# Six attention and feed-forward layers on one core: the weighted values are computed transposed, and the weights are divided by their sums before them

## The reference

```python
sim = jnp.einsum('bhwie,bhwje->bhwij', bq, bk2) * QK_SCALE   # 32 queries x 64 keys
sim = jnp.where(mask, -jnp.finfo(sim.dtype).max, sim)
attn = jax.nn.softmax(sim, -1)
out = jnp.einsum('bhwij,bhwje->bhwie', attn, bv2)
...
return out.transpose(0, 2, 1, 3).reshape(b, n, INNER) @ Wo
```

## Time and profile before

| | |
|---|---|
| median of 3 runs | 3407.45 us |
| the profiled execution, its own time | 3406.7 us |
| its span | 3405.0 us |
| TensorE matmul busy | 3269.8 us, 96% |
| VectorE busy | 2966.7 us, 87% |
| ScalarE busy | 2734.6 us, 80% |
| GpSimd busy | 2616.7 us, 77% |
| granted TensorE clock, mean | 0.988 |

### The profile page before, as it was taken

How to read it: one execution, slowest core, us unless ns; L and a number is a source line. 1 busy time by engine, 2 the same in 40 slices (tenths; PEclk the granted TensorE clock), 3 DMA queues, 4 the chain that set the end, 5 groups by cost and what they waited for, 6 DMA issues and landing times.

```text
span 3405.0 us, 161393 instructions
## 1 busy us (share of the span) xinstructions
PE 3269.8 (96%) x66106; PEld 2794.3 (82%) x66106; DVE 2966.7 (87%) x5352; ACT 2734.6 (80%) x4522; POOL 2616.7 (77%) x3360
## 2 busy tenths in 40 slices
PE   7999679999999999999999999999999999999996
PEld 5767458888888888888888888888888888888885
DVE  7777578999999999989999899999999999999995
ACT  4777458888888888888888888888888888888884
POOL 5677567777877777877778887788777878878774
PEclk9999889999999999999999999999999999999998
DMA  2000013222233222233222332222232222232221
GB/s 61 5 8 8 16 51 101 70 66 69 67 81 98 65 70 65 75 80 90 71 64 73 80 93 69 66 69 74 76 92 69 67 74 74 69 94 66 74 75 51
DMA packets 161952, 228.51 MB, mean 67 GB/s; under 512 B 42297, under 2 KB 60673, under 8 KB 161665
## 3 DMA queue, kind: packets, MB, share of 16 engines
q1 hardware_dynamic: 161792, 226.85, 24.8%
HBM read 21.00 MB, written 4.19 MB: 7 GB/s over the span
## 4 chain that ended last, share of the span: by engine, by line
POOL 38%; issue 32%; PE 15%; POOLq 2%; DVE 1%; ACT 1%; SPq 0%; DVEq 0%; ACTq 0%; DMA 0%
POOL by_cos L1253 12%; POOL by_cos L1259 9%; POOL newton_b L1239 2%; POOL newton_b L1241 2%; POOL norms L1243 2%; POOL newton_b L1237 2%; POOL xs_lob L1267 2%; POOL xn_lob L1278 2%; PE ring L1376 2%; POOL f_rstdb L1291 2%; PE ring L1430 2%; PE score L1395 1%; PE ring L1416 1%; PE proj L1367 1%; POOLq L1059 1%
## 5 line engine op out<-in xcount | busy, mean ns | idle before, releaser
L1253 POOL TENSOR_TENSOR by_cos<-by_cos,by_sin 128x1024 f32<-128x1024 f32 x384 | 914.4, 2391 | 0.0
L1259 POOL TENSOR_TENSOR by_cos<-by_cos,norms 128x1024 f32<-128x1024 f32 x384 | 729.8, 1912 | 0.0
L1653 DVE TENSOR_TENSOR by_cos<-proj,turns 128x512 f32<-128x512 f32 x768 | 524.3, 683 | 71.9 <-ACT squares L1539 67.4
L1367 PE MATMUL proj<-qkv_hi,xs_hib 128*128 128x512 f32 x1152 | 559.9, 486 | 25.6 <-DVE by_sin L1655 12.9
L1655 DVE TENSOR_TENSOR by_sin<-proj,turns 128x512 f32<-128x512 f32 x768 | 522.0, 680 | 0.0
L1539 ACT ACTIVATE squares<-proj 128x512 f32<-128x512 f32 x768 | 442.7, 593 | 41.4 <-DVE sumsb L1659 16.1
L1659 DVE TENSOR_REDUCE sumsb<-squares 128x16 f32<-128x1024 f32 x384 | 464.2, 1209 | 0.0
L1369 PE MATMUL proj<-qkv_hi,xs_lob 128*128 128x512 f32 x1152 | 457.2, 397 | 0.0
L1368 PE MATMUL proj<-qkv_lo,xs_hib 128*128 128x512 f32 x1152 | 456.7, 396 | 0.0
L1376 PE MATMUL ring<-ident,by_cos 128*128 128x128 f32 x3072 | 405.5, 275 | 7.8 <-ACT pTb L1518 4.5
L1376 PEld LDWEIGHTS ring<-ident,by_cos 128*128 128x128 f32 x3072 | 351.4, 141 | 56.4 <-issue 9.4
(11 more groups left out here) (191 smaller groups left out, 7846.5 us busy)
## 6 DMA issues: line engine op xcount, KB each, us to landing
v_win<-vb SPq DMA_DIRECT2D x1152, 128.0 KB
v_win<-vb SPq DMA_DIRECT2D x768, 64.0 KB
in_qkv<-L_ffn_Wqkv SPq DMA_DIRECT2D x12, 768.0 KB
wo<-L_ffn_Wo SPq DMA_DIRECT2D x6, 512.0 KB, 4.0
x_tok<-L_attn_x SPq DMA_DIRECT2D x8, 256.0 KB, 4.4
residual<-x_tok SPq DMA_DIRECT2D x8, 256.0 KB, 2.0
in_w<-L_ffn_W SPq DMA_DIRECT2D x12, 170.5 KB
in_qkv<-residual SPq DMA_DIRECT2D x1, 1536.0 KB, 7.3
```

What stands on the lines that cost most here:

```text
L1253: nc.gpsimd.tensor_tensor(both, both, by_sin[:, j, :], ALU.add).then_inc(e[f"{w_}_added"].sem, 1)
L1259: nc.gpsimd.tensor_tensor(heads, heads, inverse, ALU.mult).then_inc(e[f"{w_}_ready"].sem, 1)
L1367: nc.tensor.matmul(out, xs_hi[:, tile], qkv_hi[:, cols], start=True, stop=False)
L1653: nc.vector.tensor_tensor(of_heads(by_cos[:, t % 2, j, cols]), heads, table(0), ALU.mult)
```

## The change

`V` has its operands swapped. The values of a window and head are now stationary (64 rows and 64 columns of the array), the exponentials move over 32 columns, and there are again 64 such matmuls a tile. The result comes out with the features on the partitions, which is what `W` needs. `O` with its eight transposes, `R` and `attnb` are gone; `EO` copies straight from the result of `V`. Since the queries no longer lie on the partitions of the result, the division by the sums has moved ahead: a new VectorE step `PN` multiplies `probs` by the reciprocals into `weightsb`, all in SBUF, and `X` transposes `weightsb`. `SB` now waits for `PN` of the tile before (not `X`), `PN` waits for `X` of the tile before. `VM` waits for the scores of its own tile, not of the one before. `Wo` is laid out by heads and loaded with two DMAs instead of one. All tables of order are new; `X` of a pass's first tile is now done one pass later.

```diff
-    "Pool": "Mk:0 XSd:2 Ak:1 N:1 FP XSd:3 Mq:1 XL Mk:1 Xl Aq:2 N:2 Ak:2 Aq:3 Mq:2",
+    "Pool": "XSd:2 N:1 Mq:1 Mk:1 XSd:3 FP Aq:2 XL N:2 Xl Ak:2 Aq:3 Mk:2 Ak:3 Mq:2",
...
-RELEASE = {"Tq": ("q_T", 1), "Tk": ("k_T", 1), "X": ("pT", 1), "V": ("attn", 1), "O": ("oT", 1), "W": ("x_mid", 1),
+RELEASE = {"Tq": ("q_T", 1), "Tk": ("k_T", 1), "X": ("pT", 1), "V": ("oT", 1), "W": ("x_mid", 1),
...
-                    wait_tile(sp, "s_full", t - 1, when)
+                    wait_tile(sp, "s_full", t, when)
...
                 elif kind == "X":
                     out = take(token, kind, t, when)
-                    wait_tile(pe, "exp", t, when)
+                    wait_tile(pe, "weights", t, when)
                     for i in range(PAIRS):
-                        last = nc.tensor.transpose(out[:, i * P:(i + 1) * P], probs[:, i, :, :].rearrange("p a k -> p (a k)"),
+                        last = nc.tensor.transpose(out[:, i * P:(i + 1) * P], weights[:, i, :, :].rearrange("p a k -> p (a k)"),
                                                    ident[:, :])
...
-                    for i in range(PAIRS):
+                    for chunk in range(HALF):
                         for n in range(WINDOWS):
                             queries = slice(n * WINDOW, (n + 1) * WINDOW)
-                            for a in range(2):
-                                rows = slice(a * KEYS, (a + 1) * KEYS)
-                                at = a * 512 + i * DH
-                                last = nc.tensor.matmul(out[queries, at:at + DH], pT[rows, i, queries],
-                                                        v_win[rows, t % 2, n, i, :], start=True, stop=True)
+                            for c_ in range(2):
+                                for a in range(2):
+                                    i, rows = c_ * HALF + chunk, slice(a * KEYS, (a + 1) * KEYS)
+                                    at = a * 512 + chunk * P + n * WINDOW
+                                    last = nc.tensor.matmul(out[c_ * DH:(c_ + 1) * DH, at:at + WINDOW],
+                                                            v_win[rows, t % 2, n, i, :], pT[rows, i, queries],
+                                                            start=True, stop=True)
                     last.then_inc(e["pv_full"].sem, 1)
-                elif kind == "O":
-                    out = take(token, kind, t, when)
-                    wait_tile(pe, "attn", t, when)
-                    for i in range(PAIRS):
-                        last = nc.tensor.transpose(out[:, i * P:(i + 1) * P], attn[:, i, :, :].rearrange("p a d -> p (a d)"),
-                                                   ident[:, :])
-                    last.then_inc(e["oT_full"].sem, 1)
...
-                    wait_tile(act, "oT_full", t, when)
+                    wait_tile(act, "pv_full", t, when)
...
                 elif kind == "SB":
-                    wait_tile(dve, "pT_full", t - 1, when)
+                    wait_tile(dve, "weights", t - 1, when)
...
-                elif kind == "R":
-                    weighted = ring[SLOT[f"V:{in_cycle('V', t)}"]][:, :].rearrange("p (a i d) -> p a i d", a=2, d=DH)
-                    inverse = recip[:, t % 2, :].rearrange("p (i a) -> p a i", a=2)
+                elif kind == "PN":
+                    wait_tile(dve, "pT_full", t - 1, when)
                     wait_tile(dve, "recip", t, when)
-                    wait_tile(dve, "oT_full", t - 1, when)
-                    wait_tile(dve, "pv_full", t, when)
-                    nc.vector.tensor_tensor(attn[:, :, :, :].rearrange("p i a d -> p a i d"), weighted,
-                                            inverse.unsqueeze(3).broadcast_to([P, 2, PAIRS, DH]),
-                                            ALU.mult).then_inc(e["attn"].sem, 1)
+                    heads = lambda x: x[:, :, :, :].rearrange("p i a k -> p (i a) k")
+                    nc.vector.tensor_tensor(heads(weights), heads(probs), recip[:, t % 2, :].unsqueeze(2)
+                                            .broadcast_to([P, H, KEYS]), ALU.mult).then_inc(e["weights"].sem, 1)
```

More of the change, by code:

```diff
@@ L947, in layer_events @@
         **each("v"), **{f"v_moved{m}": Events(sem(f"v_moved{m}"), 160, LEAD + 1) for m in range(PER)},
-        **each("masked", "s_full", "row_max", "shifted", "exp", "denom", "recip", "pT_full", "pT", "pv_full", "attn"),
-        **each("oT_full", "oT"),
+        **each("masked", "s_full", "row_max", "shifted", "exp", "denom", "recip", "weights", "pT_full", "pT", "pv_full", "oT"),
         **once("w_full", "x_mid", "xf", "mean_full", "centred", "f_square", "var_full", "f_var", "f_rstd", "spread_full", "xn", "xn_hi",
@@ L1190, in step @@
                         sp.sem_inc(sp_ready, 1)
-                    sp.dma_start(wo[:, :, :], w["Wo"][bass.ds(new, 1)].rearrange("a (c p) n -> p (a c) n", p=P))\
-                        .then_inc(wo_loaded, 16)
+                    for c_ in range(2):
+                        half = w["Wo"][bass.ds(new, 1), c_ * INNER // 2:(c_ + 1) * INNER // 2, :]
+                        sp.dma_start(wo[c_ * DH:(c_ + 1) * DH, :, :], half.rearrange("l (u d) n -> d (l u) n", d=DH))\
+                            .then_inc(wo_loaded, 16)
             def new_layer(layer):
@@ L1216, in _ @@
             sp.wait_ge(loaded, DEPTH * 16 * LOADS)
-            sp.wait_ge(wo_loaded, DEPTH * 16)
+            sp.wait_ge(wo_loaded, DEPTH * 32)
         @block.gpsimd
@@ L1429, in step @@
                     for i in range(PAIRS):
-                        last = nc.tensor.matmul(out[:, 0:HS], wo[:, i, :], attnT[:, i, :], start=(i == 0),
+                        a, chunk = i // HALF, i % HALF
+                        last = nc.tensor.matmul(out[:, 0:HS], wo[:, 2 * chunk + a, :], attnT[:, i, :], start=(i == 0),
                                                 stop=(i == PAIRS - 1))
@@ L1578, in step @@
                         wait_pair(act, "w_full", t - 1, when)
-                    wait_tile(act, "oT_full", t, when)
-                    copy(attnT[:, :, (t % PER) * P:(t % PER + 1) * P], ring[SLOT[f"O:{in_cycle('O', t)}"]][:, :].rearrange("p (i n) -> p i n", n=P))\
+                    wait_tile(act, "pv_full", t, when)
+                    copy(attnT[:, :, (t % PER) * P:(t % PER + 1) * P], ring[SLOT[f"V:{in_cycle('V', t)}"]][:, :].rearrange("p (i n) -> p i n", n=P))\
                         .then_inc(e["oT"].sem, 1)
                 elif kind == "NO":
-                    act.wait_ge(wo_loaded, new * 16 + 16)
+                    act.wait_ge(wo_loaded, new * 32 + 32)
                 elif kind[:3] == "hi_":
```

10 lines of the change are left out of this document (3 added, 7 removed), and 37 rows, old and new, of tables (CYCLE, LAST, NEXT_WEIGHTS).

## The result

The changed kernel takes **3510.03 us**, the median of 4 runs (3506.15 to 3515.28), against 3408.43 for the kernel before (median of 4). The ratio is 1.030, with a 95% interval of 1.0281 to 1.0318: slower by 102 us. I had forecast 3367 us, faster, with a range up to 3500. The side is wrong, and the time lies 10 us outside the range.

What follows compares the result with a forecast made beforehand. TensorE bound the kernel at 30.02 us a pass and would need 29.10; VectorE, 27.04 + 2.12 + 0.45 = 29.61, would take over. Saving 0.41 us over 96 passes gives 3367 us, range 3275 to 3500.

Steps and rivals of the forecast that it cites:

- The 1.74 us for `O`: TensorE: dropping the transposes `O` frees 0.87 us each, two a pass, 1.74 us, all on the path.
- The block was put at 1.82 us: TensorE: the swapped `V` takes 1.82 us instead of 1.41, four 64x64 loads at once; 0.82 us more a pass.
- 0.89 ns a column: TensorE: cost of loading one stationary column, from 190 ns for 128 and 105 for 32; 57 ns for 64.
- few tiles: Slower rival: `V` on TensorE takes 2.9 us, pass 31.26, 119 us more, 3526 us; chance 0.12.
- light: Faster rival: `V` stays at 1.41 us, `PN` waits little; 167 us less, 3240 us; chance 0.15.
- the mutual hold: At `PN`: VectorE and GpSimd each hold the other off for a whole instruction; adds 2.12 us a pass to VectorE.
- The price without a hold: VectorE: undisturbed, `PN` costs what `R` costs, about 1.2 us, so VectorE gains nothing.
- the first wait: A pass's first `PN` meets GpSimd's `Mq:1`: some 1.25 us, taken as 1.2, less 0.14 of start-up.
- the second wait: A pass's second `PN` falls anywhere in a row of GpSimd instructions: half of one, taken as 1.2 us; ends 0 and 2.39.
- the waits that I kept: VectorE: old waits for the squares stay whole, 0.45 us a pass; those for scores and `mean` are dropped.
- priced at nothing: GpSimd (25.8 us a pass), ScalarE (25.51), `EX`, `VM` and the two `Wo` loads: covered or rare, 0 us.
- Long holds: Slower rival: each `PN` regularly waits 1.9 us for GpSimd; pass 31.0 us, 95 us more, 3502 us; chance 0.26.

Runs made afterwards that it cites:

- the kernel with one input: Changed kernel with the division left out: VectorE copies probs into weightsb by a tensor_reduce with a single SBUF input; 3340.72 us, ratio 0.9804.

## Why the prediction was wrong

**TensorE.** The 1.74 us for `O` nearly held: with the swapped block at its measured price the sum gives 29.74 for the mean pass, and the kernel with one input has 29.69. That they agree so closely is partly luck: for an ordinary pass the sum gives 29.47, and that kernel has 29.13. The block was put at 1.82 us and takes 2.00. That the width of the stationary side sets its pace was right (half the stationary columns take it to 1.22). That four loads run at a time was not shown, and the runs speak against such a count: with 32 columns, four places of the array take 1.22 us and eight take 1.25. Nor was 0.89 ns a column firm, since the 128-column loads of the transposes last 141 ns and not 190. The error is 0.36 us a pass, and not what failed: *few tiles* (2.9) and *light* (1.41) are both out.

**VectorE: the mutual hold** was the right mechanism, and that the 16 numbers a row are no protection is now measured. The price without a hold, 1.22 us, held. So did the first wait: it meets `Mq:1` and has a mean of 2.18 us, where 1.22 + 1.2 - 0.14 is 2.28.

**The step that failed: the second wait.** I wrote that a request "falls anywhere into such a row" and took half an instruction. It does not fall anywhere. Both lists are released by the same work of ScalarE, in all 70 passes that meet so (timelines of ScalarE, GpSimd and VectorE):

```profile
2510.49 0.31 ACT L1546 ACTIVATE norms<-floors,guess_bias 128x32 f32<-128x32 int32 x1
2510.71 1.02 ACT L1514 ACTIVATE pTb<-ring 128x1024 f32<-128x1024 f32 x1
2511.61 0.60 ACT L1535 ACTIVATE squares<-proj 128x512 f32<-128x512 f32 x1
...
2510.89 0.24 POOL L1237 TENSOR_TENSOR newton_b<-norms 128x32 f32<-128x32 f32 x1 [0.24 <-ACT norms L1546]
...
2512.24 0.69 DVE L1649 TENSOR_TENSOR by_cos<-proj,turns 128x512 f32<-128x512 f32 x1 [0.64 <-ACT squares L1535]
```

GpSimd waits for the guess `IG:2`, which ends at 2510.80. VectorE waits for the squares `aQq:3`, two places behind this guess in ScalarE's list. From there neither engine waits for another before the meeting: GpSimd reaches `Ak:3` 9.82 to 9.86 us behind the end of the guess, VectorE the division 9.84 to 9.85. So the worst case, a start with an addition of 2.39 us, comes back in nearly every pass: 3.21 us and not the 2.28 that I had. I had worked out the first meeting in this way, and should have done so for the second; even so, a difference of 0.01 us in the mean between two sums of nearly 10 could not have been told beforehand, and the two ends of the wait, 0 and 2.39, should both have stayed in the range at their full weight. Both divisions together take 5.39 us, 0.8 more than forecast, and 5.60 in ordinary passes.

**A second step that failed: the waits that I kept.** I left VectorE 0.45 us a pass for the squares. In an ordinary pass it is idle for 1.08 us (1.11 in the kernel with the second division one place earlier): 0.64 for the squares, 0.21 ahead of `floors` (the last step of `Rk`), and 0.24 ahead of `SB`, the sums and the reciprocals. Those ahead of `floors` and the reciprocals stood in the trace of before with the same size (18.5 and 6.2 us there, 17.8 and 6.0 here), and I had left them out without a reason.

For an ordinary pass the sum is then this. VectorE is busy for 29.93 us where I had 29.16, and idle for 1.08 where I had 0.45: 31.02 in place of 29.61. The waits alone, 0.63, would have turned the forecast of -0.41 us into +0.22; the 0.77 of busy time carries it to the +0.99 that was measured.

**Two smaller things.** I compared with one pass of 30.02 us, which is an ordinary one in length, but VectorE's 27.04 in it is low: the 30.02 us behind it, from 2529.32 on, have 27.37. And I priced only ordinary passes. Those at the turns of the layers, where the new tables also give GpSimd three of a layer's six `lo_` pieces in place of two, add the last 0.14 us to the difference of the means.

**GpSimd, ScalarE, `EX`, `VM`, `Wo`**, priced at nothing, cost nothing that shows in ordinary passes: with one input in SBUF the kernel reaches TensorE's sum. At the turns of the layers GpSimd does cost something, as told above. The gap of 3.7 us on GpSimd ahead of `N:1` looks like a cost and is none.

**The rivals.** *Long holds* is what happened, with 0.26. Its working gave 31.0 us a pass for two waits of 1.9, and ordinary passes last 31.0. That the number fits is luck: the measured waits (the division less 1.22, and the 0.14 of start-up added back) are about 1.1 and 2.1, a sum of 3.2 instead of 3.8, and its 0.45 us of idle time was too small by about as much.

**Why the expectations of the moves failed.** Each time I counted only VectorE's microseconds. A division ahead of a rotated half delays TensorE's next projection, and TensorE takes everything behind it late; the move that left all halves in place (one place earlier) is the one that gave its full value.

## What to carry to other kernels

Before a VectorE instruction is given two inputs in SBUF beside a busy GpSimd, follow both lists from the last event that they share and see which long instruction it meets; a meeting like this repeats in every pass, and where it lies within a tenth of a microsecond of an instruction's start, price both outcomes. When an engine is to become the bound, keep every wait that it has now unless the change removes its cause: here the small ones came to 0.63 us a pass, more than the gain of 0.41 that was hoped for. And before a step is moved ahead of an instruction that an in-order engine waits for, price the delay there: twice it took back most of the gain.

## What the runs showed of the hardware

- A broadcast second input of 16 numbers a row is enough for the mutual hold: 1.215 us alone, up to 3.467. The same copy with one input in SBUF stays at 1.202 to 1.221, and a multiplication with one input in PSUM and one in SBUF at 1.205 to 1.227, both with GpSimd busy beside it.
- Where both engines start within 0.04 us of each other, GpSimd went first in all 70 of such passes (divisions of over 3.4 us). In four passes the division started 0.07 to 0.08 us ahead of the addition; it took 1.22 us, and the addition 3.36. A request made 0.73 us behind the start of GpSimd's previous instruction was served at that one's end, ahead of GpSimd's next.
- For small tiles the stationary side is the dear one. 64 stationary by 32 moving columns: 15.6 ns for each load and matmul; 32 by 64: 11.0; 32 by 32: 9.5 to 9.8, on four places of the array and on eight. One load lasts 105 ns for 32 columns, 135 for 64, and 141 (transposes) or 188 to 191 (the rest) for 128, so its length is not in proportion to the columns, and several overlap.
